# Four queues reordered around the expert pipeline: the gather on GpSimd, the row loads on SyncE, the splits on VectorE, and the seam between attention and experts

## Chip, core and metric

The kernel runs on one core of one Trainium2 chip. The metric is the device time of one execution in microseconds; before the change it is 954.54 us, the median of 3 runs (951.21 to 954.67).

## What is computed

16 batches of 256 tokens of width 512 go through gated cross attention and then a mixture of 8 experts with two experts per token. All is float32.

```
x = x + tanh(g_xattn) * attention(layernorm(x), ctx)         # one head, d = 512
n = layernorm(x)
probs = softmax(n @ gate_w + gate_b, over the tokens)        # 8 experts
vals, idx = top_k(probs, 2)
h = relu(n @ w1[e] + b1[e]); h = relu(h @ w2[e] + b2[e]); y = relu(h @ w3[e] + b3[e])
v[e] = sum over tokens of y * weight(token, e)
x = x + tanh(g_ffn) * (sum of v[e] over the two experts of a token)
```

## The kernel before

Every float32 product is made as three products of a high and a low half (`hi*hi`, `lo*hi`, `hi*lo`), with operands of type fp32r. ScalarE writes the high half, and VectorE or GpSimd subtracts it to get the low half. `split_product` (L1319 to L1321) issues the three matmuls, and so nearly all matmuls stand in these three lines.

**Stage 1, the batches.** A software pipeline over 16 batches does scores, softmax, values, the second layernorm and the gate. The rows after the layernorm (`xn2`, shown as `xn`) go to HBM as `xn2_dram`. DVE finds the two best experts (`two_best`) and the slot of each token (`slots`), and GpSimd scatters pairs of token and weight into `slot_pair`.

**Stage 2, the tiles.** The slots of an expert are cut into tiles of 352 rows; here there are 24 tiles, 0 to 23. Tile m goes through these steps:

- SP loads the slot list (`load_idx(m)`), GpSimd gathers the rows into the single buffer `xg` (`gather(m)`, three indirect DMAs at L664).
- From tile 4 on, SP stores `xg` to `rows_dram` (`store_rows(m)`, L531 and L532), reads it back as four quarters `xq` (`load_quarters(m)`, L541), and DVE makes the transposed tile `et` out of it (`transpose_blocks(m)`, L1195). Tiles 0 to 3 are transposed on PE (`row_transposes`, L1549).
- ACT makes `et_hi`, DVE `et_lo`. Three layers follow on PE, each of 48 matmuls in two halves. After layers 1 and 2, ACT writes `h` with relu, a half at a time, DVE writes `h_hi` (`h_high(n, m)`, L1190) and GpSimd `h_lo` (`h_low(n, m)`, two instructions at L674). n is 0 after layer 1 and 1 after layer 2. After layer 3, DVE sums the weighted rows (`weighted_sum(m)`, L1212 to L1233) and signals `part_done` at L1226.
- The weights of a tile come by `load_w(n, m)` (only if the expert changes; 1 MB), are split by ACT (`split_w`, L825) and DVE (`w_low(n, m)`, L930).

The engines run in-order queues that are written by hand. In the loop over j, PE does layer 2 of tile j, layer 1 of tile j+1, layer 3 of tile j. `layer2_half(m)` waits until both low halves of `h_lo` after layer 1 are there:

```
need(pe, h_los[0], 2 * (m + 1))
```

GpSimd does `h_low(1, j)`, `h_low(0, j+1)`, `gather(j+3)`. The gather must not overwrite rows that are not stored yet, and so it waits:

```
need(pool, idx_in, 16 * TH * (m + 1))
need(pool, rows_out, 32 * (m - BY_BLOCKS))     # store_rows(m - 1) has landed
```

ACT does `split_w(2, j)`, relu of layer 2, `split_w(1, j+1)`, relu of layer 1, `split_w(0, j+2)`, `et_high(j+2)`. The loop begins with tile 2; what comes ahead of it is written out, and there the last batches and the first tiles are interleaved (the seam). The last four tiles are also written out.

Of the kernel before, what the change touches and what calls it, by code (L numbers as in the profile page):

```python
# [92 lines left out]
def has_tile(ahead, left):  # L93

    return ahead < left


def flamingo_block(nc, x, x_t, ctx_t, g_xattn, g_ffn, wq_t, wk_t, wv, gate_w, gate_b,
# [15 lines left out]
    with ExitStack() as ctx:  # L114
# [287 lines left out]
        def _(sp):  # L402
# [140 lines left out]
            def tile(j, left):  # L543
                if has_tile(1, left):
                    load_w(2, j + 1)
                    load_b(1, j + 1)
                if has_tile(2, left):
                    load_w(1, j + 2)
                    load_b(0, j + 2)
                if has_tile(3, left):  # L550
                    load_w(0, j + 3)
                    if not isinstance(j, int):
                        store_rows(j + 3)
                if has_tile(1, left):
                    load_b(2, j + 1)
                    load_wb(j + 1)
                if has_tile(3, left) and not isinstance(j, int):
                    load_quarters(j + 3)
                if has_tile(4, left):
                    load_idx(j + 4)  # L560

            tile(0, AHEAD + 1)
            tile(1, AHEAD + 1)
# [16 lines left out]
        def _(pool):  # L580
# [117 lines left out]
            def tile(j, left):  # L698
                if has_tile(0, left):
                    h_low(1, j)  # L700
                if has_tile(1, left):
                    h_low(0, j + 1)
                if has_tile(3, left):
                    gather(j + 3)

            tiles = tiles_in_use(pool)
            pool.wait_ge(xn2_out, 16 * B)
# [9 lines left out]
        def _(act):  # L717
# [104 lines left out]
            def split_w(n, m):  # L822
                act.wait_ge(w_in[n], W_IN[n] * (m + 1))
                need(act, l_done[n], 2 * m)
                act.activation(w_hi[n][:], w_raw[n][:], ACT.Copy).then_inc(w_his[n], 1)  # L825
# [15 lines left out]
                relu_half(n, m, 0)  # L841
                relu_half(n, m, 1)

            def et_high(m):
                need(act, l_done[0], 2 * m)
                if not isinstance(m, int):
                    act.wait_ge(et_ready, m - BY_BLOCKS + 1)
                    act.activation(et_hi[:], et[:], ACT.Copy).then_inc(et_his, TH)
                    return
                for c, (a, n) in enumerate(CHUNKS):  # L850
                    act.wait_ge(te_done, TH * m + c + 1)
                    act.activation(et_hi[:, :, a:a + n], row_banks(m)[c][:, 0:DC * n].rearrange("p (c s) -> p c s", c=DC),
                                   ACT.Copy).then_inc(et_his, 1)
# [4 lines left out]
            v_high(B - 1)  # L858
            pt_high(B - 1)
            gt_high(B - 2)  # L860
            et_high(0)
            split_w(0, 0)
            gate_exp(B - 2)
            split_w(1, 0)
            act.wait_ge(b_in[0], 16)
            relu_half(0, 0, 0)
            norm2(B - 1)
            relu_half(0, 0, 1)
            et_high(1)
            gt_high(B - 1)  # L870
            split_w(0, 1)
# [32 lines left out]
        def _(dve):  # L904
# [276 lines left out]
                dve.wait_ge(w_his[n], m + 1)  # L1181
                low(w_lo[n][:], w_raw[n][:], w_hi[n][:], w_los[n])

            def h_high(n, m):
                need(dve, l_done[n + 1], 2 * m)
                if n == 1 and isinstance(m, int) and m == 0:
                    dve.wait_ge(gate_done, B)
                for k in range(2):
                    dve.wait_ge(relu_done[n], DC * m + 2 * k + 2)
                    dve.tensor_copy(h_hi[n][:, 2 * k:2 * k + 2], h[:, 2 * k:2 * k + 2]).then_inc(h_his[n], 1)  # L1190

# [3 lines left out]
                dve.transpose(et[:].rearrange("p k (g b) -> p g k b", b=QB),  # L1195
                              xq[:].rearrange("p g (i k) -> p g k i", k=DC)).then_inc(et_ready, 1)

            def et_low(m):
                if not isinstance(m, int):
                    dve.wait_ge(et_his, TH * (m + 1))  # L1200
                    dve.tensor_tensor(et_lo[:], et[:], et_hi[:].bitcast(F32), ALU.subtract).then_inc(et_los, TH)
                    return
                for c, (a, n) in enumerate(CHUNKS):
                    dve.wait_ge(et_his, TH * m + c + 1)
                    low(et_lo[:, :, a:a + n], row_banks(m)[c][:, 0:DC * n].rearrange("p (c s) -> p c s", c=DC),
                        et_hi[:, :, a:a + n], et_los)

            def weighted_sum(m, last=False):
# [4 lines left out]
                dve.tensor_reduce(wsum[:], wb[:, :, 1], AX_X, ALU.add).then_inc(wsum_step, 1)  # L1213
                dve.wait_ge(wsum_step, 2 * m + 2)
                for oc in range(DC):
                    if last:
# [21 lines left out]
            slots(B - 3, (B - 3) % 2)  # L1238
            v_pt_low(B - 1)
            gt_low(B - 2)  # L1240
            et_low(0)
            w_low(0, 0)
            gate_softmax(B - 2)
            attended(B - 1)
            w_low(1, 0)
            h_high(0, 0)
            two_best(B - 2)
            et_low(1)
            gt_low(B - 1)
# [8 lines left out]
            slots(B - 1, (B - 1) % 2)  # L1258
            w_low(0, 2)
            et_low(2)  # L1260
            weighted_sum(0)
            w_low(2, 1)
            h_high(1, 1)
# [2 lines left out]
            h_high(0, 2)  # L1266
            w_low(0, 3)
            et_low(3)
            weighted_sum(1)

            def tile(j, left):
                if has_tile(0, left):
                    w_low(2, j)
                    h_high(1, j)
                if has_tile(1, left):
                    w_low(1, j + 1)
                    h_high(0, j + 1)
                if has_tile(2, left):
                    if not isinstance(j, int):
                        transpose_blocks(j + 2)  # L1280
                    w_low(0, j + 2)
                    et_low(j + 2)
                if has_tile(0, left):
                    weighted_sum(j, last=(left == 1))

            tiles = tiles_in_use(dve)
            tile_pipeline(dve, tile, tiles)
# [25 lines left out]
        def _(pe):  # L1313
# [240 lines left out]
            scores(B - 1)  # L1554
            gate_transposes(B - 3)
            values(B - 1, 0)
            ranks(B - 3)
            values(B - 1, 1)
            pt_transposes(B - 1)
            xn2_transposes(B - 2)  # L1560
            need(pe, qa_los, 2 * B)
            row_transposes(0, range(2))
            gate_logits(B - 2)
            row_transposes(0, range(2, TH))
            p_times_v(B - 1)
            layer1_half(0, 0)
            gate_transposes(B - 2)
            layer1_half(0, 1)
# [92 lines left out]
```

## Time and profile before

| what | value |
|---|---|
| median of 3 runs | 954.54 us |
| the profiled execution | 953.95 us, of which the span is 952.2 us |
| busy PE / DVE / ACT / POOL | 918.2 / 721.6 / 419.5 / 454.7 us |
| granted TensorE clock, mean | 0.981 of full speed |

PE is the engine that is nearly always busy; the others have room. So what counts is where PE stands still, where its clock is below full, and who lets it go on. In the timeline a row is one instruction or a merged run of them, with the start, the duration and, in square brackets, the idle time ahead of it on its engine and who ended it.

### The profile page before, as it was taken

To read this page: it belongs to the slowest core of one execution; us is meant where nothing else is said; L and a number is where in the kernel's file an instruction comes from. 1 tells how busy PE (TensorE), PEld (TensorE's weight loads), DVE (VectorE), ACT (ScalarE), POOL (GpSimd) and SP (SyncE) were. 2 spreads that over 40 slices of the span, in tenths; PEclk is the share of its full clock that TensorE was granted. 3 is DMA by queue.
4 is the path that set the end of the run, shared out by engine and by line. 5 is a ranking of instruction groups with operands and counts; after the bars stand their busy time and mean duration, and the time that the engine had idled before them with its cause. 6 is when DMAs were issued, how large, how long until landed. Compare 5 with 4: busy or idle time off the path is not lost.

```text
span 952.2 us, 18810 instructions
## 1 busy us (share of the span) xinstructions
PE 918.2 (96%) x5746; PEld 863.7 (91%) x5746; DVE 721.6 (76%) x1379; ACT 419.5 (44%) x594; POOL 454.7 (48%) x402
## 2 busy tenths in 40 slices
PE   9999999999999979999999999999999999999985
PEld 6989888899888869899999999999999999999981
DVE  5667787887888867876877786889877777777646
ACT  5454443544433455344444444444444444444311
POOL 4225444444434566653655453655544554455213
PEclk9999999999999998999999999999999999999995
DMA  6433322233211544446656777866565555564008
GB/s 233 155 114 110 130 91 88 93 127 115 106 66 67 143 128 84 135 90 184 184 165 172 208 215 221 239 222 184 133 173 158 150 154 148 150 185 119 17 16 352
DMA packets 91924, 138.67 MB, mean 146 GB/s; under 512 B 28528, under 2 KB 56944, under 8 KB 88688
## 3 DMA queue, kind: packets, MB, share of 16 engines
q1 hardware_dynamic: 84464, 120.86, 42.8%
q0 software_dynamic: 7424, 17.38, 6.2%
q8 instruction: 18, 0.29, 0.1%
q14 instruction: 18, 0.15, 0.1%
HBM read 106.66 MB, written 31.53 MB: 145 GB/s over the span
## 4 chain that ended last, share of the span: by engine, by line
PE 65%; issue 11%; POOL 7%; DVE 6%; DMA 5%; SPq 4%; ACT 1%; POOLq 0%; DVEq 0%; ACTq 0%
PE bank L1319 20%; PE bank L1320 19%; PE bank L1321 19%; POOL h_lo L674 4%; POOL xg L664 3%; DMA rows_dram<-xg 2%; DMA xg<-xn_dram,idx 2%; DVE x_all L1309 2%; PE bank L1333 1%; PE bank L1390 1%; SPq L541 1%; PE bank L1431 1%; DMA idx<-slot_pair 1%; SPq L463 1%; PE bank L1433 1%
## 5 line engine op out<-in xcount | busy, mean ns | idle before, releaser
L674 POOL TENSOR_TENSOR h_lo<-h,h_hi 128x704 fp32r<-128x704 f32 x96 | 183.6, 1916 | 245.2 <-DVE h_hi L1190 245.2
L1319 PE MATMUL bank<-h_hi,w_hi 128*128 128x352 f32 x752 | 245.7, 327 | 7.3 <-POOL h_lo L674 4.1
L1321 PE MATMUL bank<-h_hi,w_lo 128*128 128x352 f32 x752 | 243.6, 324 | 0.0
L1320 PE MATMUL bank<-h_lo,w_hi 128*128 128x352 f32 x752 | 242.6, 323 | 0.0
L930 DVE TENSOR_TENSOR w_lo<-w_raw,w_hi 128x2048 fp32r<-128x2048 f32 x72 | 181.0, 2514 | 22.4 <-ACT w_hi L825 18.0
L836 ACT ACTIVATE h<-bank,bias 128x352 f32<-128x352 f32 x192 | 95.8, 551 | 201.0 <-PE bank L1321 170.8
L825 ACT ACTIVATE w_hi<-w_raw 128x2048 fp32r<-128x2048 f32 x72 | 137.8, 1916 | 54.6 <-PE bank L1321 46.0
L1319 PEld LDWEIGHTS bank<-h_hi,w_hi 128*128 128x128 f32 x752 | 142.1, 189 | 9.6 <-issue 9.6
L1320 PEld LDWEIGHTS bank<-h_lo,w_hi 128*128 128x128 f32 x752 | 142.1, 189 | 0.0
L1321 PEld LDWEIGHTS bank<-h_hi,w_lo 128*128 128x128 f32 x752 | 141.7, 188 | 0.0
L1319 PE MATMUL bank<-et_hi,w_hi 128*128 128x352 f32 x384 | 125.0, 326 | 4.5 <-DVE part L1226 2.6
L1190 DVE CAST h_hi<-h 128x704 fp32r<-128x704 f32 x96 | 69.1, 725 | 76.3 <-ACT h L836 76.3
L1320 PE MATMUL bank<-et_lo,w_hi 128*128 128x352 f32 x384 | 123.7, 322 | 0.0
L1321 PE MATMUL bank<-et_hi,w_lo 128*128 128x352 f32 x384 | 123.7, 322 | 0.0
L664 POOL DMA_INDIRECT xg<-xn_dram,idx x72 | 104.5, 1452 | 36.6 <-issue 16.6
L634 POOL DMA_INDIRECT slot_pair<-pair,slot_u x64 | 66.1, 1033 | 36.5 <-DVE pair L987 19.3
L1319 PEld LDWEIGHTS bank<-et_hi,w_hi 128*128 128x128 f32 x384 | 72.5, 189 | 5.5 <-issue 3.1
L1320 PEld LDWEIGHTS bank<-et_lo,w_hi 128*128 128x128 f32 x384 | 72.7, 189 | 0.0
L1321 PEld LDWEIGHTS bank<-et_hi,w_lo 128*128 128x128 f32 x384 | 72.6, 189 | 0.0
L601 POOL TENSOR_SCALAR rn<-mv 128x2 f32<-128x2 f32 x32 | 9.4, 293 | 131.1 <-DVE mv L927 131.1
L1319 PE MATMUL bank<-xt_hi,a_hi 128*128 128x256 f32 x240 | 69.1, 288 | 0.0
L1195 DVE STREAM_TRANSPOSE et<-xq 128x1408 f32<-128x1408 f32 x20 | 54.8, 2739 | 17.5 <-DMA xq<-rows_dram 17.4
(202 smaller groups left out, 1767.1 us busy)
## 6 DMA issues: line engine op xcount, KB each, us to landing
w_raw<-in_w SPq DMA_DIRECT2D x24, 1024.0 KB, 5.1
xq<-rows_dram SPq DMA_DIRECT2D x80, 176.0 KB, 4.1
w_raw<-in_w SPq DMA_DIRECT2D x48, 256.0 KB, 6.1
rows_dram<-xg SPq DMA_DIRECT2D x20, 512.0 KB, 3.1
wb<-slot_pair SPq DMA_DIRECT2D x24, 352.0 KB, 4.1
xt_raw<-in_x_t SPq DMA_DIRECT2D x16, 512.0 KB, 3.9
c_raw<-in_ctx_t SPq DMA_DIRECT2D x16, 512.0 KB, 3.3
x_all<-in_x SPq DMA_DIRECT2D x16, 512.0 KB, 4.8
```

Source lines behind the costliest of these rows:

```text
L634: pool.indirect_dma_start(slot_pair, bass.IndirectOffsetOnAxis(ap=slot_u[:, k, n:n + 1], axis=0), pair[:, k, n], None).then_inc(pair_sent[ ...
L664: pool.indirect_dma_start(xg[0:n, c], None, rows, bass.IndirectOffsetOnAxis(ap=idx[0:n, c, 0:1], axis=0)).then_inc(gathered, 16)
L674: pool.tensor_tensor(h_lo[n][:, 2 * k:2 * k + 2], h[:, 2 * k:2 * k + 2], h_hi[n][:, 2 * k:2 * k + 2].bitcast(F32), ALU.subtract).then_inc( ...
L825: act.activation(w_hi[n][:], w_raw[n][:], ACT.Copy).then_inc(w_his[n], 1)
L836: act.activation(h[:, oc], layer_banks(n, m)[oc][:, 0:TILE], ACT.Relu, bias=bias[n][:, oc:oc + 1]).then_inc(relu_done[n], 1)
L930: dve.tensor_tensor(dst, src, hi.bitcast(F32), ALU.subtract).then_inc(done, 1)
L1190: dve.tensor_copy(h_hi[n][:, 2 * k:2 * k + 2], h[:, 2 * k:2 * k + 2]).then_inc(h_his[n], 1)
L1195: dve.transpose(et[:].rearrange("p k (g b) -> p g k b", b=QB), xq[:].rearrange("p g (i k) -> p g k i", k=DC)).then_inc(et_ready, 1)
L1309: dve.tensor_tensor(row, bank[n % 8][:], row, ALU.add).then_inc(res_dve, 1)
L1319: pe.matmul(out_ap, lh, rh, start=(i == 0), stop=False)
L1320: pe.matmul(out_ap, lh, rl, start=False, stop=False)
L1321: last = pe.matmul(out_ap, ll, rh, start=False, stop=(i == n - 1))
```

## The change

It moves instructions and adds none to the loop but for the numbers they carry. On SP the loop now stores rows and loads the slot list and the quarters first and the weights of layer 1 and the combine weights after; in the written-out tiles 0 and 1, `load_idx` moves ahead of `load_w(0, ...)`. On GpSimd the gather stands between the two `h_low`. On DVE `w_low(0, j+2)` stands ahead of the block transposes, and the first two instructions of `weighted_sum` (now `weights_of`) ahead of `et_low`. In the seam, the ranks of batch 13 are put between two halves of `values(15, 1)`, `gate_logits(14)` behind `p_times_v(15)`, the third chunk of `et_high(0)` and `et_low(0)` behind the weight split, the first half of `h_high(0, 0)` ahead of `w_low(1, 0)`, and the relu of the second half ahead of `norm2(15)`.

```
@@ SP, tile(j, left)
                 if has_tile(2, left):
                     load_w(1, j + 2)
                     load_b(0, j + 2)
+                if has_tile(3, left) and not isinstance(j, int):
+                    store_rows(j + 3)
+                if has_tile(4, left):
+                    load_idx(j + 4)
                 if has_tile(3, left):
+                    if not isinstance(j, int):
+                        load_quarters(j + 3)
                     load_w(0, j + 3)
-                    if not isinstance(j, int):
-                        store_rows(j + 3)
                 if has_tile(1, left):
                     load_b(2, j + 1)
                     load_wb(j + 1)
-                if has_tile(3, left) and not isinstance(j, int):
-                    load_quarters(j + 3)
-                if has_tile(4, left):
-                    load_idx(j + 4)
@@ POOL, tile(j, left)
                 if has_tile(0, left):
                     h_low(1, j)
+                if has_tile(3, left):
+                    gather(j + 3)
                 if has_tile(1, left):
                     h_low(0, j + 1)
-                if has_tile(3, left):
-                    gather(j + 3)
@@ ACT, seam
-            et_high(0)
+            et_high(0, range(2))
             split_w(0, 0)
+            et_high(0, range(2, TH))
             gate_exp(B - 2)
             split_w(1, 0)
             act.wait_ge(b_in[0], 16)
             relu_half(0, 0, 0)
+            relu_half(0, 0, 1)
             norm2(B - 1)
-            relu_half(0, 0, 1)
@@ DVE, seam
             gt_low(B - 2)
-            et_low(0)
+            et_low(0, range(2))
             w_low(0, 0)
+            et_low(0, range(2, TH))
             gate_softmax(B - 2)
             attended(B - 1)
+            h_high(0, 0, range(1))
             w_low(1, 0)
-            h_high(0, 0)
+            h_high(0, 0, range(1, 2))
@@ DVE, tile(j, left)
                 if has_tile(2, left):
+                    w_low(0, j + 2)
                     if not isinstance(j, int):
                         transpose_blocks(j + 2)
-                    w_low(0, j + 2)
+                    weights_of(j)
                     et_low(j + 2)
-                if has_tile(0, left):
-                    weighted_sum(j, last=(left == 1))
+                else:
+                    weights_of(j)
+                weighted_sum(j, last=(left == 1))
@@ PE, seam
             values(B - 1, 0)
-            ranks(B - 3)
-            values(B - 1, 1)
+            values_with_ranks(B - 1, 1, B - 3)
             pt_transposes(B - 1)
             xn2_transposes(B - 2)
             need(pe, qa_los, 2 * B)
-            row_transposes(0, range(2))
+            row_transposes(0)
+            p_times_v(B - 1)
             gate_logits(B - 2)
-            row_transposes(0, range(2, TH))
-            p_times_v(B - 1)
             layer1_half(0, 0)
```

GpSimd's queue in the body of the loop, before; the first pair of `h_lo` is that after layer 2 of tile j, the second that after layer 1 of tile j+1:

```order
L674 TENSOR_TENSOR h_lo<-h,h_hi 128x704
L673 REGISTER_ALU
L674 TENSOR_TENSOR h_lo<-h,h_hi 128x704
L673 ISA
L674 TENSOR_TENSOR h_lo<-h,h_hi 128x704
L673 REGISTER_ALU
L674 TENSOR_TENSOR h_lo<-h,h_hi 128x704
L41 ISA x2
L664 DMA xg<-xn_dram,idx 128x512 x2
L664 DMA xg<-xn_dram,idx 96x512
```

The same place of the changed kernel:

```order
L674 TENSOR_TENSOR h_lo<-h,h_hi 128x704
L673 REGISTER_ALU
L674 TENSOR_TENSOR h_lo<-h,h_hi 128x704
L41 ISA x2
L664 DMA xg<-xn_dram,idx 128x512 x2
L664 DMA xg<-xn_dram,idx 96x512
L673 ISA
L674 TENSOR_TENSOR h_lo<-h,h_hi 128x704
L673 REGISTER_ALU
L674 TENSOR_TENSOR h_lo<-h,h_hi 128x704
```

The three gathers, with their waits, now stand ahead of the second pair.

DVE's queue in the body of the loop, before, from the second half of `h_high(0, j+1)` on:

```order
L1190 CAST h_hi<-h 128x704
L1193 ISA
L41 REGISTER_ALU
L1195 STREAM_TRANSPOSE et<-xq 128x11x4x32
L1181 REGISTER_ALU
L930 TENSOR_TENSOR w_lo<-w_raw,w_hi 128x2048
L1200 REGISTER_ALU
L1201 TENSOR_TENSOR et_lo<-et,et_hi 128x1408
L1210 REGISTER_ALU
L1212 TENSOR_SCALAR nb<-bias 128x4
L1213 TENSOR_REDUCE wsum<-wb 128x1
```

The same place of the changed kernel, whose DVE lines are numbered two higher:

```order
L1192 CAST h_hi<-h 128x704
L1183 REGISTER_ALU
L932 TENSOR_TENSOR w_lo<-w_raw,w_hi 128x2048
L1195 ISA
L41 REGISTER_ALU
L1197 STREAM_TRANSPOSE et<-xq 128x11x4x32
L1212 REGISTER_ALU
L1214 TENSOR_SCALAR nb<-bias 128x4
L1215 TENSOR_REDUCE wsum<-wb 128x1
L1202 REGISTER_ALU
L1203 TENSOR_TENSOR et_lo<-et,et_hi 128x1408
```

The weight split has changed places with the transposes, and between the transposes and `et_lo`, where ACT makes `et_hi`, only the two small instructions are left.

SP's queue ahead of the loop, before: behind the combine weights of tile 2 come the slot list of tile 5 and the store of tile 4:

```order
L496 DMA wb<-slot_pair 128x704
L488 TENSOR_LOAD table
L488 ISA x2
L490 ISA
L490 DMA idx<-slot_pair 128x2
L490 ISA
L490 DMA idx<-slot_pair 128x2
L490 ISA
L490 DMA idx<-slot_pair 96x2
L388 TENSOR_LOAD extra
L388 ISA x2
L531 DMA rows_dram<-xg 128x2x512
```

The same place of the changed kernel, from the last of the weights' four quarters for layer 1 of tile 4 on:

```order
L463 DMA w_raw<-in_w 32x4x512
L470 UNCONDITIONAL_BRANCH
L472 UNCONDITIONAL_BRANCH
L481 TENSOR_LOAD table
L481 ISA x2
L482 ISA
L482 DMA bias<-in_b 128x4
L495 TENSOR_LOAD table
L495 ISA x2
L496 ISA
L496 DMA wb<-slot_pair 128x704
L388 TENSOR_LOAD extra
```

The slot list of tile 5 (`load_idx(5)`, which waits for the gather of tile 4) has gone ahead of the weights; weights, bias and combine weights now stand between it and the store.

## Rows read from the trace of the kernel before

**Rows 1.** Who waited for whom, on PE, from 420 us to the end
```profile
PE bank L1319 <- POOL h_lo L674: 4.1, 4, 1.4
...
PE bank L1319 <- DVE part L1226: 2.6, 2, 1.3
```

**Rows 2.** Who waited for whom, whole span: engine, line, releaser: us, times, longest
```profile
DVE et L1195 <- DMA xq<-rows_dram: 17.4, 7, 5.0
```

**Rows 3.** Timeline of PE in the seam: the waits that the change touches
```profile
335.57 0.31 PE L1429 MATMUL bank<-gt_hi,gw 128*40 128x256 f32 x1 [0.92 <-DVE gt_lo L930]
341.87 0.43 PE L1319 MATMUL bank<-et_hi,w_hi 128*128 128x352 f32 x1 [1.93 <-DVE w_lo L930]
357.68 0.20 PE L1379 MATMUL bank<-ind,tri_half 128*128 128x16 bf16 x1 [2.59 <-DVE ind L1053]
```

**Rows 4.** Stretches: length, busy us (and instructions) of PE, PEld, DVE, ACT, POOL; PEclk, DMA share, GB/s
```profile
358.20:363.40 5.20, 5.20 (x19) 5.20 (x19) 5.06 (x15) 2.55 (x2) 2.67 (x4) 0.51 0.49 144
660.00:720.00 60.00, 60.00 (x377) 60.00 (x376) 46.60 (x52) 28.44 (x32) 32.21 (x19) 1.00 0.58 157
```

**Rows 5.** Timeline of SP and POOL ahead of the loop, and of DVE and PE after
```profile
413.53 2.92 SPq L463 DMA_DIRECT2D w_raw<-in_w  x4
416.35 0.92 POOL L664 DMA_INDIRECT xg<-xn_dram,idx  x1 [0.30 <-issue]
419.26 0.34 SPq L496 DMA_DIRECT2D wb<-slot_pair  x1
425.69 1.47 SPq L490 DMA_DIRECT2D idx<-slot_pair  x3
428.12 0.40 SPq L531 DMA_DIRECT2D rows_dram<-xg  x1
431.88 1.85 SPq L541 DMA_DIRECT2D xq<-rows_dram  x4
438.19 0.32 PE L1319 MATMUL bank<-h_hi,w_hi 128*128 128x352 f32 x1
```

**Rows 6.** Timeline of one tile of the loop, PE and ACT
```profile
738.91 0.32 PE L1319 MATMUL bank<-h_hi,w_hi 128*128 128x352 f32 x1
739.11 1.00 ACT L836 ACTIVATE h<-bank,bias 128x352 f32<-128x352 f32 x2 [2.81 <-PE bank L1321]
740.00 1.92 ACT L825 ACTIVATE w_hi<-w_raw 128x2048 fp32r<-128x2048 f32 x1
743.44 1.39 ACT L848 ACTIVATE et_hi<-et 128x1408 fp32r<-128x1408 f32 x1 [1.52 <-DVE et L1195]
```

**Rows 7.** The same tile on DVE and POOL
```profile
740.14 0.53 DVE L1190 CAST h_hi<-h 128x704 fp32r<-128x704 f32 x1 [2.53 <-ACT h L836]
743.26 2.26 DVE L930 TENSOR_TENSOR w_lo<-w_raw,w_hi 128x2048 fp32r<-128x2048 f32 x1
745.42 1.63 DVE L1201 TENSOR_TENSOR et_lo<-et,et_hi 128x1408 fp32r<-128x1408 f32 x1
747.68 0.59 DVE L1221 SCALAR_TENSOR_TENSOR bank<-bank,nb,wb 128x352 f32<-128x352 f32 x1
751.39 2.29 DVE L930 TENSOR_TENSOR w_lo<-w_raw,w_hi 128x2048 fp32r<-128x2048 f32 x1 [0.20 <-issue]
740.75 1.72 POOL L674 TENSOR_TENSOR h_lo<-h,h_hi 128x704 fp32r<-128x704 f32 x1 [1.36 <-DVE h_hi L1190]
742.61 0.97 POOL L664 DMA_INDIRECT xg<-xn_dram,idx  x1
743.89 2.46 POOL L664 DMA_INDIRECT xg<-xn_dram,idx  x1 [0.30 <-issue]
```

**Rows 8.** Another tile: a low half behind a weight split, and layer 3's start
```profile
665.14 2.29 DVE L930 TENSOR_TENSOR w_lo<-w_raw,w_hi 128x2048 fp32r<-128x2048 f32 x1
665.25 3.75 POOL L674 TENSOR_TENSOR h_lo<-h,h_hi 128x704 fp32r<-128x704 f32 x1 [0.47 <-DVE h_hi L1190]
669.73 0.32 PE L1319 MATMUL bank<-h_hi,w_hi 128*128 128x352 f32 x1
```

More of the change, by code:

```diff
@@ L842, in relu, with et_high @@
                 relu_half(n, m, 1)
-            def et_high(m):
+            def et_high(m, chunks=range(TH)):
                 need(act, l_done[0], 2 * m)
@@ L849, in et_high @@
                     return
-                for c, (a, n) in enumerate(CHUNKS):
+                for c in chunks:
+                    a, n = CHUNKS[c]
                     act.wait_ge(te_done, TH * m + c + 1)
@@ L1182, in w_low, with h_high @@
                 low(w_lo[n][:], w_raw[n][:], w_hi[n][:], w_los[n])
-            def h_high(n, m):
+            def h_high(n, m, halves=range(2)):
                 need(dve, l_done[n + 1], 2 * m)
@@ L1187, in h_high @@
                     dve.wait_ge(gate_done, B)
-                for k in range(2):
+                for k in halves:
                     dve.wait_ge(relu_done[n], DC * m + 2 * k + 2)
@@ L1196, in transpose_blocks, with et_low @@
                               xq[:].rearrange("p g (i k) -> p g k i", k=DC)).then_inc(et_ready, 1)
-            def et_low(m):
+            def et_low(m, chunks=range(TH)):
                 if not isinstance(m, int):
@@ L1202, in et_low @@
                     return
-                for c, (a, n) in enumerate(CHUNKS):
+                for c in chunks:
+                    a, n = CHUNKS[c]
                     dve.wait_ge(et_his, TH * m + c + 1)
@@ L1206, in et_low, with weights_of @@
                         et_hi[:, :, a:a + n], et_los)
-            def weighted_sum(m, last=False):
+            def weights_of(m):
                 dve.wait_ge(b_in[2], 16 * (m + 1))
@@ L1213, in weighted_sum @@
                 dve.tensor_reduce(wsum[:], wb[:, :, 1], AX_X, ALU.add).then_inc(wsum_step, 1)
+            def weighted_sum(m, last=False):
                 dve.wait_ge(wsum_step, 2 * m + 2)
@@ L1260, in _ @@
             et_low(2)
+            weights_of(0)
             weighted_sum(0)
@@ L1268, in _ @@
             et_low(3)
+            weights_of(1)
             weighted_sum(1)
@@ L1373, in values, with values_with_ranks @@
                 split_product(bV[c][:], cols(c_hi, c_lo, c * P, P), cols(wv_hi, wv_lo, 0, D), v_done)
+            def values_with_ranks(m, c, ranked):
+                need(pe, x2_done, 2 * m)
+                for i in range(DC):
+                    if i == DC // 2:
+                        ranks(ranked)
+                    ch, cl = c_hi[:, i, c * P:(c + 1) * P], c_lo[:, i, c * P:(c + 1) * P]
+                    pe.matmul(bV[c][:], ch, wv_hi[:, i], start=(i == 0), stop=False)
+                    pe.matmul(bV[c][:], ch, wv_lo[:, i], start=False, stop=False)
+                    last = pe.matmul(bV[c][:], cl, wv_hi[:, i], start=False, stop=(i == DC - 1))
+                last.then_inc(v_done, 1)
             def ranks(m):
```

## The prediction

> **What bounds the kernel now.** I read first where PE stands still, since it is busy for 918.2 of 952.2 us. In the table of waits from 420 us on, the loop gives PE two waits: 4.1 us in four places for `h_lo`, 2.6 us in two for `part_done` [rows 1]. That is 6.7 us in all, and a stretch in mid-loop has none: 377 matmuls in 60 us at full clock, so 0.159 us each, 7.64 us for a layer and 22.9 us for a tile [rows 4]. The 6.7 us are DVE running late: it waits 17.4 us for `xq` in seven places [rows 2], and what stands behind that wait comes late. In the seam the change touches three waits of PE: 0.92, 1.93 and 2.59 us [rows 3]. After the last, the stretch from 358.2 to 363.4 shows a granted clock of 0.51 and 19 matmuls in 5.2 us, where 33 fit at full clock [rows 4]: 1.2 GHz instead of 2.4, which costs 14 x 0.159 = 2.2 us.
>
> So at most some 5.4 + 2.2 + 6.7 = 14.3 us are to be had. What may be lost isn't bounded so, since three queues of the loop change.
>
> **The seam.** The wait of 0.92 goes, since p_times_v now stands ahead of the gate's product. That of 1.93 is for the first weight split; ACT makes that split ahead of the third chunk, and so it comes about 2 us earlier, but so does PE. That of 2.59 is for the two best experts of batch 14, which DVE still finds behind `attended(15)`; nothing is taken out of that chain but the late start of its head. Bounds: nothing gained, or all of 5.4 + 2.2 = 7.6 us. I take 3 us, the 0.9 and the 2 us by which the head comes earlier, and leave the slow clock as it is.
>
> **The first tile of the loop.** Here the new orders of SP and GpSimd meet. Today's rows [rows 5]: the last DMA of gather(4) is issued by 416.35 + 0.92 = 417.3; the slot list of tile 5, which waits for its landing, follows at 425.7, so 8.4 us later, while 1 MB of weights issued from 413.5 to 416.4 is in flight. In the new order these weights come behind the slot list. Without them I take 5.3 us for landing and issue (an estimate; 8.4 is the upper bound), and the slot list goes at 422.6. Behind it: 1.5 us for the list, 2.9 for the four quarters of the weights, 2.8 for bias and combine weights (416.45 to 419.26), 1.0 to the store (427.16 to 428.12), and about 2.1 to read the table and branch ahead of the weights (an estimate). The store is at 432.9, not 428.1. Today the quarters follow the store by 3.8 us, since they wait for its landing, and so `rows_out` comes at about 436.5.
>
> gather(5) waits for it, and now `h_low(0, 3)` is queued behind gather(5). An indirect DMA takes 0.97 us and 0.3 between two [rows 7], so 3.5 for three; two `h_lo` take 3.6 with their gap: 443.6, and 0.24 more to PE. One clash with the split `w_low(0, 4)`, which falls here, adds about 1. PE wants to start layer 2 of tile 3 at 438.19 [rows 5] and gets it at about 444.8: 6.6 us. (All on today's clock; the gain of the seam moves both.) Bounds: 5.5 if nothing clashes, 9.5 if the list comes as late as now. A wait so much longer than 2.59 will be followed by the slow clock too, 2.2 us: together 8.8. On the other side the first two waits of rows 1's kind vanish, as DVE has that time to catch up, and later ones too, as rows are stored some 7 us earlier in a tile: minus 6.7 (bounds: minus 4, 0 if they recur).
>
> **A tile in the steady loop.** Take L for the end of layer 1, when layer 3 starts (738.91 [rows 6]). Today: relu L+0.2 to 1.2, `h_hi` L+1.2 to 1.8, the second `h_lo` L+1.8 to 3.6, the gather after it [rows 7]. PE needs it at L+7.6; 4 us are spare. Two things use them up.
>
> First DVE. `w_low(0)` stood behind the transposes (at L+4.35, after 2.6 us of them) and covered ACT's 1.39 us of `et_hi`. In the new order it waits for ACT's split, which ends at 740.00 + 1.92 = L+3.0 [rows 6], and DVE is idle for 1.2 us; it ends at L+5.3, the transposes at L+8.0, `et_hi` at L+9.5 (with 0.16 of handing over), `et_lo` at L+11.1. From the end of `et_lo` to the next tile's `w_low(2)` it is 751.39 - 747.05 = 4.3 us today, of which the moved pair is 0.6 [rows 7]; so that starts at L+14.8, not L+12.5. DVE is 2.3 us later with `h_high(1)`. The second `h_lo` after layer 2 then meets `w_low(1)` already queued, and it waits for it: it took 3.75 us for 1.7 and ended 0.7 us ahead of layer 3 [rows 8].
>
> Second GpSimd. So the gather starts at about L-0.6, not L-3.8, and ends at L+3.0. At that moment `w_low(0)` starts on DVE, too. The rows show that a split and an `h_lo` don't overlap [rows 8]; in whichever order, one split of 2.26 and two `h_lo` of 1.72 with a gap of 0.15 follow: L+3.0+5.85 = L+8.9, and 0.24 to PE: L+9.1. PE needs it at L+7.6. That is 1.4 us per tile; if the split starts first. If `h_lo` does, it is about the same, but DVE is 1.8 us later, and the next layer 3 waits for about 1 more. Lower bound 0: a tile in which the gather starts at L-3.8 ends just in time. I take 1.3, below the 1.4 that a tile by itself gives, since some will slip through. It applies to tiles 4 to 21, those with a gather ahead of their low half: 18 x 1.3 = 23.4 us. As these waits are no longer than those in [rows 1] after which the clock stayed at full, no slow clock is added.
>
> **Sum.** 953.95 - 3 + 8.8 - 6.7 + 23.4 = 976.5 us against the profiled execution; the median of before lies 0.6 higher, so 977.
>
> The Trainium skill, page "SBUF — State Buffer", section "Who interferes with whom", says that a two-input operation takes only the read side of the pair of ports that DVE and GpSimd share, and infers that it doesn't hold up the descriptors of a gather. The trace has it otherwise here: a gather DMA issued at 743.89 took 2.46 us, until 0.8 after the split that began at 743.26 had ended, against 0.97 for the one ahead of it [rows 7].
>
> **Rivals.** (1) The steady loop loses little, 0 to 0.6 us per tile: if the gather is ready by L+1.2, both `h_lo` can be done before `w_low(0)` starts. For it speaks that PE's next start moves by the wait itself, which gives the others time; against it the 2.3 us of DVE, which are in every tile. It gives 953.95 - 3 + 8.8 - 6.7 + (0 to 11) = 953 to 964. By the skill's rule above the gather is never held by a split, and this would be the case. (2) Faster: the gather fits between the pairs, SP's chain for tile 5 is done before 438, as the landing of gather(4) is quick and the table reads are short, and the seam gives more. It decides at a start of gather(5) by 434, 4.2 us before PE needs the second half of `h_lo`; my chain gives 436.5. With no steady loss, it is 953.95 - 3 - 6.7 = 944, and 940 with the slow clock gone. (3) Worse: `h_lo` goes first in every second tile, (1.3 + 2.1) / 2 = 1.7 us per tile, and weights that are now loaded 5 us later come late for ACT where experts change: 984 to 995.
>
> **How the numbers follow.** I give my forecast (964 to 988) 0.56, rival (1) 0.22, rival (2) 0.14, rival (3) 0.08. About 0.5% (4.8 us) is what this kernel's measurement can tell from no change. Slower by more: 0.56 + 0.08 and two thirds of rival (1), 0.79; the same: the rest of (1), 0.07; faster: 0.14. The likeliest case's own range is 964 to 988. The range that leaves out no more than 2 in 10 begins at 953, the lower end of (1), and ends at 990.
>
> **What would show it.** In the changed profile, PE's waits for `h_lo` go from 4.1 us to 25 to 35, most of them at the start of layer 2, with periods of 24 us instead of 22.9; the first, at the start of layer 2 of tile 3, is the longest, with a granted clock near 0.5 after it. GpSimd's rows show the three gathers between the pairs, and the first gather of the loop waits for `rows_dram`. DVE's 17.4 us for `xq` shrink below 8, and it waits for ACT's `w_hi` instead. The waits of 0.92 and 1.93 in the seam are gone or smaller. I am wrong if the second pair of `h_lo` ends before L+7.4 in most tiles, that is if the split and the pair don't meet, or if ACT makes `w_hi` sooner than at L+3.

## The result, and the profile after

The changed kernel takes **996.49 us** (median of 6 runs, 991.18 to 1002.79); before, 953.85 us (6 runs, 949.10 to 954.67). The ratio is 1.0456, with a 95% interval of 1.041 to 1.0502. I had forecast 977, range 953 to 990: the sign was right, and about half of the loss was seen (22.5 us of 42.6). The times of kernels are medians over runs in the chip's usual, fast state; one of the four runs of e15 below (995.58 us) was in its slower state and is left out.

The page's first lines, span and busy time of each engine:

```profile
span 996.8 us, 18809 instructions
...
PE 935.8 (94%) x5746; PEld 877.1 (88%) x5746; DVE 792.5 (80%) x1379; ACT 416.1 (42%) x594; POOL 460.9 (46%) x402
```

PE stands still for 996.8 - 935.8 = 61.0 us, before for 34.0: 27 us more. And it is busy for 17.6 us more with the same 5746 matmuls: some of these ran on a lower clock, as shown below. DVE is busy for 71 us more with the same 1379 instructions. So they took longer, and the groups of the costliest instructions say which (count | busy, mean ns | idle before):

```profile
L932 DVE TENSOR_TENSOR w_lo<-w_raw,w_hi 128x2048 fp32r<-128x2048 f32 x72 | 228.2, 3169 | 31.5 <-ACT w_hi L825 27.1 <-issue 4.3
L674 POOL TENSOR_TENSOR h_lo<-h,h_hi 128x704 fp32r<-128x704 f32 x96 | 220.5, 2313 | 286.4 <-DVE h_hi L1192 286.1
...
L1192 DVE CAST h_hi<-h 128x704 fp32r<-128x704 f32 x96 | 92.0, 972 | 37.6 <-ACT h L836 37.2
...
L664 POOL DMA_INDIRECT xg<-xn_dram,idx x72 | 74.4, 1034 | 36.0 <-issue 16.4 <-DMA idx<-slot_pair 9.3 <-DMA rows_dram<-xg 8.7
```

And the same groups before:

```profile
L674 POOL TENSOR_TENSOR h_lo<-h,h_hi 128x704 fp32r<-128x704 f32 x96 | 183.6, 1916 | 245.2 <-DVE h_hi L1190 245.2
...
L930 DVE TENSOR_TENSOR w_lo<-w_raw,w_hi 128x2048 fp32r<-128x2048 f32 x72 | 181.0, 2514 | 22.4 <-ACT w_hi L825 18.0
...
L1190 DVE CAST h_hi<-h 128x704 fp32r<-128x704 f32 x96 | 69.1, 725 | 76.3 <-ACT h L836 76.3
...
L664 POOL DMA_INDIRECT xg<-xn_dram,idx x72 | 104.5, 1452 | 36.6 <-issue 16.6
```

The splits take 47 us more and the casts 23: together nearly all of DVE's 71. GpSimd's `h_lo` takes 37 us more and its gathers 30 less. Alone, split, `h_lo` and cast take 2.26, 1.72 and 0.53 us [rows 7]. The waits from 420 us on, those that answer to [rows 1], and two of DVE and ACT:

```profile
ACT et_hi L848 <- DVE et L1197: 147.9, 20, 9.9
...
PE bank L1329 <- DVE part L1230: 24.2, 12, 2.2
DVE et_lo L1203 <- ACT et_hi L848: 18.9, 20, 1.1
...
PE bank L1329 <- POOL h_lo L674: 11.3, 11, 4.2
```

I had expected 25 to 35 us of waits for `h_lo` at layer 2. There are 11.3, and the greater part is for `part_done`, at the start of layer 1, which my working had left out. One tile of the loop, in the order of time (from four engines' timelines; here and in the later ones only the rows that are spoken of):

```profile
740.15 1.92 ACT L825 ACTIVATE w_hi<-w_raw 128x2048 fp32r<-128x2048 f32 x1
741.25 0.93 POOL L664 DMA_INDIRECT xg<-xn_dram,idx  x1 [0.30 <-issue]
742.10 5.61 DVE L932 TENSOR_TENSOR w_lo<-w_raw,w_hi 128x2048 fp32r<-128x2048 f32 x1 [1.28 <-ACT w_hi L825]
742.20 3.36 POOL L674 TENSOR_TENSOR h_lo<-h,h_hi 128x704 fp32r<-128x704 f32 x2
747.63 2.68 DVE L1197 STREAM_TRANSPOSE et<-xq 128x1408 f32<-128x1408 f32 x1
750.41 1.38 ACT L848 ACTIVATE et_hi<-et 128x1408 fp32r<-128x1408 f32 x1 [8.34 <-DVE et L1197]
751.90 1.63 DVE L1203 TENSOR_TENSOR et_lo<-et,et_hi 128x1408 fp32r<-128x1408 f32 x1 [1.11 <-ACT et_hi L848]
756.18 0.22 DVE L1230 SCALAR_TENSOR_TENSOR part<-bias,wsum,acc 128x4 f32<-128x4 f32 x1
756.55 0.40 PE L1329 MATMUL bank<-et_hi,w_hi 128*128 128x352 f32 x1 [1.91 <-DVE part L1230]
```

Layer 3 started at 739.07, which is L. The gather ends at L+3.1 and the split is ready at L+3.0, as forecast. But the pair of `h_lo` takes its two turns at once (3.36 us), and the split gets none between them: it ends 5.61 us after its start. Everything behind it is late: transposes, `et_hi` with nothing beside it, `et_lo`, the sum. PE wants layer 1 at L+15.6 and gets it at L+17.5. There are 12 such waits in the loop, of 1.89 to 2.18 us. After nine of them the granted clock goes to its lower level for part of the next 5 us (mean 0.66, so some 1.7 us lost); after three (705.88, 756.55 and 807.05) it stays at full, and these three waits are no shorter. Stretches of 5 us from the start of a layer 1, without and with it (length, then PE's busy us and matmuls; PEclk is the third number from the end):

```profile
756.50:761.50 5.00, 4.95 (x31) 4.99 (x32) 4.75 (x6) 0.98 (x1) 1.55 (x1) 1.00 0.22 73
...
884.70:889.70 5.00, 4.95 (x21) 4.99 (x22) 4.87 (x6) 0.70 (x1) 1.67 (x1) 0.66 0.30 71
```

Ten matmuls fewer are 1.6 us. From the fifth start of a layer 1 to the last there are 19 periods; they add up to 489.8 us (446.6 to 936.4, 25.8 each), against 445.4 before (23.4 each). An undisturbed tile takes 23.06 us, so 51.7 us of the 489.8 are lost: 24.2 in the 12 waits for `part_done`, some 15 on the lower clock behind them, 6.6 in waits for `h_lo`; I can't place the last 5 or 6. Against before it is 44.4 us: nearly all of the profiled difference of 44.6 us lies in the loop, as what the seam gains and the first loop tile loses about cancel.

### The profile page after: what moved, and what is told of

The parts are those of the page before. It is cut to its first block, busy times and chain, and to the rows that moved or that the text cites. A ratio compares the mean times of both kernels' runs of the same rounds, so it can differ in the third digit from the quotient of the medians.

```text
span 996.8 us, 18809 instructions
## 1 busy us (share of the span) xinstructions
PE 935.8 (94%) x5746; PEld 877.1 (88%) x5746; DVE 792.5 (80%) x1379; ACT 416.1 (42%) x594; POOL 460.9 (46%) x402
## 4 chain that ended last, share of the span: by engine, by line
PE 39%; issue 34%; POOL 13%; DVE 6%; DMA 3%; ACT 2%; SPq 1%; POOLq 0%; DVEq 0%; ACTq 0%
PE bank L1329 11%; PE bank L1330 11%; PE bank L1331 11%; POOL h_lo L674 8%; POOL xg L664 4%; DVE x_all L1319 2%; PE bank L1343 1%; DVE et L1197 1%; DMA xg<-xn_dram,idx 1%; PE bank L1412 1%; ACT w_hi L825 1%; DMA idx<-slot_pair 1%; PE bank L1453 1%; ACT et_hi L848 1%; DVE bank L1225 1%
## 5 line engine op out<-in xcount | busy, mean ns | idle before, releaser
L674 POOL TENSOR_TENSOR h_lo<-h,h_hi 128x704 fp32r<-128x704 f32 x96 | 220.5, 2313 | 286.4 <-DVE h_hi L1192 286.1
L1329 PE MATMUL bank<-h_hi,w_hi 128*128 128x352 f32 x752 | 246.8, 328 | 14.3 <-POOL h_lo L674 11.3
L932 DVE TENSOR_TENSOR w_lo<-w_raw,w_hi 128x2048 fp32r<-128x2048 f32 x72 | 228.2, 3169 | 31.5 <-ACT w_hi L825 27.1
L1329 PE MATMUL bank<-et_hi,w_hi 128*128 128x352 f32 x384 | 131.1, 342 | 25.6 <-DVE part L1230 24.2
L1331 PE MATMUL bank<-et_hi,w_lo 128*128 128x352 f32 x384 | 129.5, 337 | 0.0
L1330 PE MATMUL bank<-et_lo,w_hi 128*128 128x352 f32 x384 | 129.5, 337 | 0.0
L1192 DVE CAST h_hi<-h 128x704 fp32r<-128x704 f32 x96 | 92.0, 972 | 37.6 <-ACT h L836 37.2
L664 POOL DMA_INDIRECT xg<-xn_dram,idx x72 | 74.4, 1034 | 36.0 <-issue 16.4
L848 ACT ACTIVATE et_hi<-et 128x1408 fp32r<-128x1408 f32 x20 | 27.7, 1384 | 147.9 <-DVE et L1197 147.9
L1331 PEld LDWEIGHTS bank<-et_hi,w_lo 128*128 128x128 f32 x384 | 77.3, 201 | 0.0
L1331 PE MATMUL bank<-xt_hi,a_lo 128*128 128x256 f32 x240 | 67.9, 283 | 0.0
```

The costliest lines, as they stand in the source:

```text
L664: pool.indirect_dma_start(xg[0:n, c], None, rows, bass.IndirectOffsetOnAxis(ap=idx[0:n, c, 0:1], axis=0)).then_inc(gathered, 16)
L674: pool.tensor_tensor(h_lo[n][:, 2 * k:2 * k + 2], h[:, 2 * k:2 * k + 2], h_hi[n][:, 2 * k:2 * k + 2].bitcast(F32), ALU.subtract).then_inc( ...
L932: dve.tensor_tensor(dst, src, hi.bitcast(F32), ALU.subtract).then_inc(done, 1)
L1329: pe.matmul(out_ap, lh, rh, start=(i == 0), stop=False)
L1330: pe.matmul(out_ap, lh, rl, start=False, stop=False)
L1331: last = pe.matmul(out_ap, ll, rh, start=False, stop=(i == n - 1))
```

## The experiments

Medians of 3 to 10 runs beside 13 to 25 runs of the kernel before on the same chip (medians 954.68 to 955.80); the first row is the result above. The ratio's 95% interval is in brackets. "Split first" is `w_low(0)` ahead of the transposes; "weights early" is `weights_of` ahead of `et_low`.

| kernel | seam | SyncE | gather between | split first | weights early | us | ratio |
|---|---|---|---|---|---|---|---|
| changed | x | x | x | x | x | 996.5 | 1.0456 (1.041 to 1.0502) |
| e15_sp_back | x | | x | x | x | 984.5 | 1.0304 (1.0266 to 1.0342) |
| e1_gather_back | x | x | | x | x | 986.9 | 1.0345 (1.0281 to 1.0409) |
| e8_weights_of_early | x | x | x | | x | 956.3 | 1.0002 (0.9973 to 1.003) |
| e2_dve_back | x | x | x | | | 958.4 | 1.0036 (1.0013 to 1.0059) |
| e7_seam_sp | x | x | | | | 958.7 | 1.0003 (0.9967 to 1.004) |
| e9_seam_weights | x | | | | x | 949.1 | 0.9935 (0.9907 to 0.9963) |
| e3_seam_only | x | | | | | 949.7 | 0.9942 (0.9907 to 0.9977) |
| e6_sp_only | | x | | | | 965.1 | 1.008 (1.0048 to 1.0111) |
| e5_dve_only | | | | x | x | 973.7 | 1.0166 (1.0103 to 1.0229) |
| e4_gather_only | | | x | | | 1000.2 | 1.0476 (1.0413 to 1.0539) |

**Undoing one of the two orders that I held to meet.** On GpSimd and on DVE, the changed kernel with

```
# e1_gather_back                     # e2_dve_back
 h_low(1, j)                         +transpose_blocks(j + 2)
-gather(j + 3)                        w_low(0, j + 2)
 h_low(0, j + 1)                     -transpose_blocks(j + 2)
+gather(j + 3)                       -weights_of(j)
                                      et_low(j + 2)
                                     +weights_of(j)
```

> The changed kernel with GpSimd's loop order of before (both h_low pairs, then the gather). Theory 'meeting': the loss comes from w_low(0) on VectorE and the h_lo pair on GpSimd, which the gather keeps back until both want to start; then the pair goes back to back and the split is stretched from 2.3 to 5.6-5.9 us. Without the gather ahead of it the pair ends before the split starts: no split over 4 us in the loop, PE's waits for part_done go from 24.2 to under 8 us, time 945 to 960. Rival 'VectorE alone': waiting for w_hi and the uncovered et_hi make VectorE the bound whatever GpSimd does: waits for part stay near 20 us and the time stays at 980 to 996.

> The changed kernel with VectorE's loop order of before (transposes, w_low(0), et_low, then the whole weighted sum). Theory 'meeting': the pair runs beside the transposes; w_low(0) starts later and meets at most its last half; waits for part_done under 8 us, time 948 to 965, and what is left is the wait for h_lo at layer 2. Rival 'gather alone': the gather ahead of the pair is itself the loss, and the time stays over 980. Rival 'VectorE alone': like the theory, 945 to 955; this run and the one with the gather put back tell these apart only together.

986.9 and 958.4. My theory fell with the first: with the gather put back, 32 us of loss are still there. No split takes over 4 us there, as I had said (3.8 at most), and PE's waits for `part_done` fall to 11.6 us, but those for `h_lo` rise to 21.4. So it is DVE's order that does most of it: 28 us without the gather between the pairs (986.9 against e7's 958.7), 38 with it (996.5 against 958.4). The gather there costs nothing without DVE's order (958.4 against 958.7), and some 10 us beside it.

**One part alone.** The seam's edits, and the move on GpSimd, each made to the kernel before.

> The kernel before with only the edits of the seam (PE, ScalarE, VectorE); the loop's orders of SyncE, GpSimd and VectorE are those of before. The changed kernel's trace has layer 2 of tile 2 at 409.83 where before had 415.03, 5.2 us earlier. If this is the seam's own work, the time is 949 (946 to 951). If part of it came from SyncE's order (the slot lists in tiles 0 and 1 ahead of the weights), it is 951 to 953.

> The kernel before with only GpSimd's order changed: the gather between the two h_low pairs. Theory 'meeting' (gather and VectorE's order are both needed): 955 to 970, with PE waiting for h_lo at layer 2 and splits of 2.3 to 4 us. Rival 'gather alone': 985 or more. Rival 'VectorE alone': 953 to 956.

The seam's 5.1 us are its own. The gather alone costs 45 us, though it costs none beside SyncE's new order. Its trace, one tile (SP, POOL, PE):

```profile
715.95 0.90 SPq L490 DMA_DIRECT2D idx<-slot_pair  x2
719.41 0.97 POOL L664 DMA_INDIRECT xg<-xn_dram,idx  x1 [3.92 <-DMA idx<-slot_pair]
723.81 3.90 POOL L674 TENSOR_TENSOR h_lo<-h,h_hi 128x704 fp32r<-128x704 f32 x2
727.84 0.66 PE L1319 MATMUL bank<-h_hi,w_hi 128*128 128x352 f32 x1 [4.07 <-POOL h_lo L674]
```

In the old order SP loads the slot list last in a tile, behind the quarters. The gather waits for it, and the second pair of `h_lo` behind the gather; PE waits 3 to 4 us in about every second tile.

> The kernel before with the gather between the pairs (1000.2 us alone) and on SyncE only the slot list of tile j+4 loaded ahead of the weights of layer 1; the store and the quarters stay where they were. In the gather-only run the gathers waited 39.4 us for the slot lists. Theory 'the late slot list is the loss': 955 to 965. Rival 'the late store of the rows is as much of it': 975 to 995, the gather then waits for rows_dram.

With `load_idx(j + 4)` moved up ahead of `load_w(0, j + 3)` and nothing else, 966.88 us (ratio 1.0125, 1.0076 to 1.0174): 33 of the 45 us are the late list. It is above the range that I gave for it, and none of the rest is a late store in the loop, since only the first gather waits for `rows_dram` (8.5 us). The first tile costs PE 3.3 us, and a tile in the steady loop takes 23.6 us instead of 23.06.

**DVE's order alone, and the rest by pairs.**

> The kernel before with only VectorE's loop order changed (w_low(0) ahead of the transposes, the two first instructions of the weighted sum ahead of et_low). Theory 'VectorE is the bound': in the run with the gather put back a tile took 24.35 us, with VectorE idle for some 2.4 us of it and its instructions stretched by some 5; that needs nothing from GpSimd's or SyncE's new order, so this run gives 954 + 20 x 1.4 = 982, 976 to 992. Rival 'SyncE's order makes it so' (weights that come later): 953 to 965.

> The kernel before with only SyncE's orders changed. Theory 'the bounds are VectorE and the gather's waits': rows are stored earlier and nothing waits for them or for the weights, so 952 to 957. Rival 'weights late': over 960, with ScalarE's splits waiting for w_raw.

> The changed kernel with the loop orders of GpSimd and of VectorE put back: only the seam and SyncE's order are new. Theory: the seam's gain of 5 us stays and SyncE's order costs nothing, 946 to 951. Rival: if SyncE's order costs something of itself, 952 to 960.

> The changed kernel with only w_low(0) put back behind the transposes; the two first instructions of the weighted sum stay ahead of et_low, and the gather between the pairs. Theory 'the place of the split': 955 to 961, as with the whole VectorE order undone (958.4). Rival 'the early weights': over 970, since nb and wsum would stand where they stretch or wait for the combine weights.

DVE's order alone: 973.7, a little under what I gave, and 19 periods of 24.35 us, nearly all alike. Below, one of them, from layer 3's start to the next (DVE, POOL, PE):

```profile
725.20 1.43 DVE L1190 CAST h_hi<-h 128x704 fp32r<-128x704 f32 x1 [0.74 <-ACT h L836]
727.01 3.55 DVE L930 TENSOR_TENSOR w_lo<-w_raw,w_hi 128x2048 fp32r<-128x2048 f32 x1 [0.38 <-ACT w_hi L825]
730.49 2.69 DVE L1195 STREAM_TRANSPOSE et<-xq 128x1408 f32<-128x1408 f32 x1
734.75 1.63 DVE L1201 TENSOR_TENSOR et_lo<-et,et_hi 128x1408 fp32r<-128x1408 f32 x1 [1.11 <-ACT et_hi L848]
740.00 2.29 DVE L930 TENSOR_TENSOR w_lo<-w_raw,w_hi 128x2048 fp32r<-128x2048 f32 x1 [0.20 <-issue]
742.80 5.61 POOL L674 TENSOR_TENSOR h_lo<-h,h_hi 128x704 fp32r<-128x704 f32 x2 [8.92 <-DVE h_hi L1190]
743.07 3.80 DVE L930 TENSOR_TENSOR w_lo<-w_raw,w_hi 128x2048 fp32r<-128x2048 f32 x1
746.80 2.00 DVE L1190 CAST h_hi<-h 128x704 fp32r<-128x704 f32 x1
748.66 0.42 PE L1324 MATMUL bank<-h_hi,w_hi 128*128 128x352 f32 x1 [0.98 <-POOL h_lo L674]
```

DVE is idle for 0.74 + 0.38 + 1.11 + 0.20 = 2.4 us of 24.3. Four instructions took longer than alone: 1.43 and 2.00 for 0.53, 3.55 and 3.80 for 2.26, together 5.2 us. So DVE's tile is longer than PE's, and PE follows. The chain that repeats isn't DVE's alone, though: ACT's relu for the last `h_hi` waits until the stretched pair of `h_lo` has left `h`, and with it ACT's `w_hi`. ACT's waits for `h_lo` from 420 us on, in e5 and before:

```profile
ACT h L836 <- POOL h_lo L674: 92.5, 40, 2.7
```

```profile
ACT h L836 <- POOL h_lo L674: 21.0, 8, 3.9
```

In e8 the split stands behind the transposes again; it is stretched there as well (5.0 us in 16 of 18 tiles), but it lies beside ACT's `et_hi`, and this split doesn't wait for `w_hi`. There PE waits 5.5 us in the loop, and the time is 956.3. So the place of the split is worth 996.5 - 956.3 = 40 us in the changed kernel, and the early weights nothing that can be told from the spread (956.3 and 958.4, 949.1 and 949.7).

SyncE's order costs 9 to 10 us by itself (958.7 against 949.7, 965.1 against 954.96), as the rival had it in both runs.

**Is it DVE's length, or the place in which the two meet?** Both kernels are e5 with less work: e10 leaves out half of the rows of the weighted sum, e11 half of each low half of `h`, where old values stay. The lines are shortened; `wb`, `h` and `h_hi` are read over the same half. In `weighted_sum` and in `h_low`, for the tiles of the loop:

```
# e10_half_sum
+n = TILE if isinstance(m, int) else TILE // 2
-z = layer_banks(2, m)[oc][:, 0:TILE]
+z = layer_banks(2, m)[oc][:, 0:n]
# e11_half_h_lo
+c = TILE if isinstance(m, int) else TILE // 2
-h_lo[n][:, 2 * k:2 * k + 2] = h - h_hi
+h_lo[n][:, 2 * k:2 * k + 2, 0:c] = (h - h_hi)[..., 0:c]
```

> The kernel with only VectorE's new loop order (973.7 us, 24.34 us per tile), but the four instructions of the weighted sum read only half of a tile's rows in the loop (176 of 352; the other half of the sum is left out). Theory 'VectorE's chain closes the loop': these four stand behind the split and the transposes and shorten the chain by some 1.1 us per tile, so the tile falls to 23.0 to 23.3 us and the time to 953 to 960. Rival 'the h_lo pair and the splits meet by their place in the tile, whatever VectorE's length': no change, 970 to 975.

> The kernel with only VectorE's new loop order (973.7 us), but GpSimd's h_lo covers half of the rows in the loop (the other half keeps old values): 0.9 us each for 1.7, 3.4 us less for GpSimd per tile. Theory: the four stretched instructions of VectorE in a tile (w_lo 3.79 and 3.56, h_hi 2.00 and 1.43) lose about half of their 5 us of excess, the tile goes back to 22.9 and the time to 950 to 954. Rival 'VectorE's idle time for w_hi and et_hi alone': 968 to 974.

959.54 us (ratio 1.004, 1.0019 to 1.0062) and 949.87 us (0.9939, 0.9907 to 0.9971). A DVE chain 1.1 us shorter gives back 14 of 19 us: periods of 23.6, where I had expected 23.0 to 23.3. A GpSimd that holds DVE up half as long gives back all: 18 of 19 periods under 23.1 us, though DVE's idle time is all there still, as the waits of e11 from 420 us on show:

```profile
DVE w_lo L932 <- ACT w_hi L827: 38.6, 40, 1.3
DVE et_lo L1203 <- ACT et_hi L850: 22.2, 20, 1.1
```

So idle time alone isn't the cause, and the clash alone isn't (e8 has it). It is the two together, on a chain that thereby gets longer than PE's 23.06 us. One thing e11 can't tell: it also shortens the pair itself, for which ACT and PE wait (ACT's 92.5 us for `h_lo` in e5 are 1.8 in e11). How much of e5's loss comes by DVE's stretching and how much straight from the longer pair isn't shown.

**What SyncE's order costs, and whether it carries the rest.** e9 has the two parts that cost nothing.

> The kernel before with the seam's edits and the two first instructions of the weighted sum ahead of et_low; the split stays behind the transposes, the orders of GpSimd and SyncE are those of before. The early weights go into the time in which VectorE waits for et_hi or the split, 0.6 us a tile off VectorE's chain: 946 to 950, since PE had only some 6 us of waits in the loop of the seam-only kernel (949.7). If they cost something, over 952.

> The kernel with the seam and SyncE's order (958.7 us), but in the written-out tiles 0 and 1 the slot list keeps its old place behind the combine weights; in the loop SyncE's order is the new one. In the 958.7 run the store ahead of the loop is issued at 429.45 against 424.67 in the seam-only run, VectorE waits 8.67 us for xq and PE 5.0 us for part_done in tile 3. Theory 'the first loop tile': that wait goes below 2 us, and the time is 953 to 955. Rival 'weights late in the whole loop': 957 to 959.

> The kernel with the seam and SyncE's order (958.7 us), but the weights of layer 1 stand ahead of the quarters in the loop (store, slot list, weights, quarters, bias, combine weights). ScalarE waited 48.2 us for w_raw in the 958.7 run, against 7.0 in the seam-only run. Theory 'the first loop tile costs most': ScalarE's waits fall below 20 us but the 5.0 us wait in tile 3 stays, 954 to 957. Rival 'late weights cost it': 949 to 952.

> The changed kernel with only SyncE's orders put back (seam, gather between the pairs, VectorE's order). The gather-only run lost 46 us, since every second tile waits 3 to 4 us for h_lo behind a gather that waits for its slot list; VectorE's order alone lost 19. Theory 'the gather needs the earlier slot list, whatever VectorE does': 995 to 1020, with waits for idx on GpSimd. Rival 'VectorE's longer tile hides the late list': 975 to 990, below the changed kernel's 996.5.

e13 has `load_idx(j + 4)` at its old place in tiles 0 and 1: 954.17 us (ratio 1.0, 0.9981 to 1.0019), 4.5 less than e7. The first loop tile, in e7 (SP, DVE, PE):

```profile
429.45 0.39 SPq L531 DMA_DIRECT2D rows_dram<-xg  x1
440.58 2.70 DVE L1197 STREAM_TRANSPOSE et<-xq 128x1408 f32<-128x1408 f32 x1 [8.67 <-DMA xq<-rows_dram]
450.72 0.63 PE L1327 MATMUL bank<-et_hi,w_hi 128*128 128x352 f32 x1 [5.00 <-DVE part L1230]
```

And in e13:

```profile
426.21 0.39 SPq L531 DMA_DIRECT2D rows_dram<-xg  x1
435.73 2.70 DVE L1199 STREAM_TRANSPOSE et<-xq 128x1408 f32<-128x1408 f32 x1 [5.85 <-DMA xq<-rows_dram]
```

PE's wait there falls from 5.0 to 2.2 us. About half of SyncE's cost is this tile. The other 4.5 us (e13 against e3) stay with the loop's order: ACT waits 43.1 us for `w_raw` in e13 and 7.0 in e3. Which tiles they are lost in, the runs don't tell. e14, with `load_w(0, j + 3)` ahead of the quarters, was to cure that: ACT's wait falls to 13.2 us, but DVE's wait for `xq` grows to 36.3 us, and the time is 965.5 (1.0124, 1.0099 to 1.0148). Rows and weights share SP's queue, and whichever is second is late; my expectation had neither case. e15 has the waits of my theory (GpSimd waits 50.9 us for `idx`) and the time of its rival: 984.5 us (979.9 to 991.4, three runs), 12 us below the changed kernel's. Once DVE's tile is the longer one, SyncE's new order saves nothing here.

The best version is the seam with or without the early weights, 949.1 and 949.7 us, 0.6% under the kernel before. Nothing that was reordered in the loop gained.

## Why the prediction was wrong

**The seam** (forecast -3): -5.1 us. Right in kind, and undersized. The waits of 0.92 and 2.59 [rows 3] are gone, that of 1.93 is now 1.34. But a wait in line behind them, for ACT's `xn`, went from 0.80 to 3.51 us, and PE's waits of over 0.3 us from 310 to 370 us fall from 8.0 to 6.1 only. The rest of the 5.2 us by which the profiled kernel is ahead after the seam is the clock, which I had left as it was. The same 40 us of the seam before, in the changed kernel (5 us earlier) and in e7, which has the same seam:

```profile
330.00:370.00 40.00, 33.76 (x191) 31.11 (x190) 26.10 (x62) 20.13 (x31) 22.93 (x20) 0.87 0.46 119
```

```profile
325.00:365.00 40.00, 35.15 (x212) 31.80 (x211) 29.30 (x80) 22.14 (x35) 25.24 (x26) 0.96 0.65 144
```

```profile
330.00:370.00 40.00, 33.98 (x192) 31.35 (x193) 30.00 (x73) 22.14 (x36) 23.87 (x20) 0.87 0.44 116
```

From 0.87 to 0.96 of 40 us is some 3.5 us. As e7 shows 0.87 again, the clock's share isn't the same in every run, and the split of the 5.1 us between waits and clock stays open.

**The first tile of the loop** (forecast +8.8): PE's wait for `h_lo` was 4.15 us, not 6.6, and ten matmuls on the lower clock followed, 1.6 us. The chain was the one that I gave, SP's order, store, gather, pair:

```profile
415.39 0.87 SPq L490 DMA_DIRECT2D idx<-slot_pair  x2
418.29 2.91 SPq L463 DMA_DIRECT2D w_raw<-in_w  x4
424.71 0.39 SPq L531 DMA_DIRECT2D rows_dram<-xg  x1
429.85 1.51 POOL L664 DMA_INDIRECT xg<-xn_dram,idx  x1 [8.73 <-DMA rows_dram<-xg]
433.85 3.32 POOL L674 TENSOR_TENSOR h_lo<-h,h_hi 128x704 fp32r<-128x704 f32 x2
437.29 0.42 PE L1329 MATMUL bank<-h_hi,w_hi 128*128 128x352 f32 x1 [4.15 <-POOL h_lo L674]
```

Layer 2 of tile 2 starts 5.2 us earlier than before; against that mark the slot list came 5.6 us after it, not 7.6. The list went 3.3 us behind the last DMA of gather(4), not 5.3, and no split fell beside the pair of `h_lo` (3.32 us), for which I had added 1. The mechanism was right; its size was some 3 us too large.

**A tile in the steady loop** (forecast -6.7 + 23.4 = +16.7): +44.4 us. This is the step that failed. I wrote that split and pair end at L+8.9 "in whichever order", took that as the end of `h_lo`, and added: "it is about the same, but DVE is 1.8 us later". The end was right; L+8.6 to L+9.0 was measured. But it was the split's end and not the pair's, in 12 of the 18 pairs behind a gather; there the pair ended at L+6.5 to L+6.8, before the L+7.4 that I had named as the sign of being wrong. Each of the 12 waits for `part_done` comes in the tile of one of these 12 pairs, and none behind the other six, where the split went first and PE waited 0.3 to 0.6 us for `h_lo`, not 1.4. My own chain of DVE had the split at L+5.3 and the sum 4.3 us behind `et_lo`; it was never worked through again with the split that the clash gives. With L+8.9 in it: transposes L+11.6, `et_hi` L+13.1, `et_lo` L+14.7, `part_done` about 2.9 behind (as in the rows above), L+17.6. PE needs it at L+15.6. The trace has `part_done`'s instruction at L+17.1. That is 2 us in 12 tiles, and the lower clock behind nine of them, where I had 1.3 us per tile; and it is at layer 1, not at layer 2.

**The independence of the tiles** was wrong as well, and by e1 this is the larger part: without the gather between the pairs no pair goes first, and DVE's order still costs 28 of its 38 us. I treated each tile as starting from today's slack, and DVE's 2.3 us of delay as reaching PE by the clash alone. DVE was idle enough for that before (busy 46.6 us of 60 [rows 4]), but the reorder lays open 2.4 us of waits for ACT and draws 5.2 us of stretching, and then DVE's period (24.35 us in e5) is over PE's 23.06 (22.9 by my sum), and no slack comes back.

**The clock.** "No slow clock is added" was wrong. It rested on waits of at most 1.4 us; the new ones are 1.9 to 2.2, and the 5 us after the one at 884.75 have a granted clock of 0.66, as shown above. Nine such stretches and that of the first tile, 1.7 us each, are 17 us and so about as much as PE's 17.6 us of more busy time. My sum had 2.2 us, for the first tile; this is the second largest miss.

**Rivals.** Rival (3), with a chance of 0.08 and 984 to 995, came nearest. It had `h_lo` going first in every second tile; it was 12 of 18. Its other half, weights late for ACT, isn't seen in the changed kernel, whose table of waits has none for `w_raw` from 420 us on. (In rival (2), 944 less the 2.2 us of slow clock is 942, not 940.) That a late slot list or store would hold the gather was weighed for the first tile alone. In the loop it is true without SyncE's order (e4, 45 us) and not with it: here SyncE's order earned what it costs. The Trainium skill ("SBUF — State Buffer", "Who interferes with whom") calls the pair of ports that DVE and GpSimd share an exclusive lock, and says that the order of issue decides who blocks. The durations agree with the lock: 5.61 us is the pair's 3.36 and the split's 2.26, with nothing overlapped. On the order the starts of the rows don't bear it out: the split's row starts 0.10 us ahead of the pair's, and it is the split that goes last.

## What to carry to other kernels

When two engines exclude each other, work the clash through both chains: whoever goes second pays, and the price goes to what stands behind it, perhaps two layers later. An instruction that seems to wait idly in a queue may be the cover of another engine's latency; before moving it, write down what DVE waits for on each side of it, add up the engine's period, and compare that with the bound's period. And a reorder of several queues is judged by parts: here one part cost 45 us alone and nothing beside another, one gained 5, and one cost 40.

## What the hardware showed that I had not expected

A split on VectorE that waits while GpSimd works through a pair of `h_lo` does not always get its turn between the two. Behind a gather, with both inputs ready, the pair took 3.35 to 3.39 us and the split 5.6 to 5.9 in 12 of the 18 such pairs of the changed kernel from 440 us on (in the other six the split went first, 4.76 us for the pair). In e8 the pair took 3.37 to 3.41 us in all 18. Where GpSimd had waited for `h_hi` just before, the turns alternate: 5.60 to 5.65 us for the pair in all 13 of the changed kernel, and 3.8 for the split in 12 of them; 5.60 to 5.62 in all 20 of e5. Why the one and not the other wasn't tried; the second subtraction being queued already may be the reason.

A cast of `h_hi` (0.53 us alone) is held up by `h_lo` as well: 1.43 to 2.04 us.

A gather's DMA instruction on GpSimd is held up by VectorE's subtractions too. It takes 0.9 to 1.3 us otherwise. From 430 us on, the kernel before has 24 that took 1.2 to 4.1 us, and e5 has 18 of 2.2 to 2.8; every one of these 42 ended 0.8 to 0.9 us behind the end of a split or of `et_lo`. The changed kernel, whose gathers end as the split starts, has none over 1.3 us. What in the instruction waits, the rows don't show.
